# Local attention's first four tiles drawn into the last eighteen block products of the attention before it

## The reference

```
# layer 0: causal attention, 16 heads of 8
q, k, v = split(x @ W_attn + b_attn)
y = softmax(causal(q @ k.T / sqrt(8))) @ v
x = layernorm(x + y @ W_proj + b_proj)
# layer 1: two blocks of local attention, 8 heads of 64, window 64
h = shift_token(x)                       # half the channels come from the token before
q, k, v = split(h @ wqkv)
q = l2norm(q) * q_scale; k = l2norm(k) * k_scale
q, k = rotary_xpos(q, k)                 # times cos and sin tables, times a scale
o = local_attention(q, k, v)             # own window and the one before
x = x + o @ wo                           # then a gated feed-forward part
```

## Time and profile before

| | us |
|---|---|
| median of 3 runs (2395.67 to 2404.09) | 2396.33 |
| the profiled execution | 2395.39 |
| its span | 2393.6 |
| TensorE busy, share of the span | 90% |
| last `take` of the first attention starts | 210.85 |
| `v` 0 of local attention starts | 241.11 |

### The profile page before, as it was taken

How to read it: one execution, slowest core, us unless ns; L and a number is a source line. 1 busy time by engine, 2 the same in 40 slices (tenths; PEclk the granted TensorE clock), 3 DMA queues, 4 the chain that set the end, 5 groups by cost and what they waited for, 6 DMA issues and landing times.

```text
span 2393.6 us, 40349 instructions
## 1 busy us (share of the span) xinstructions
PE 2157.5 (90%) x15552; PEld 1245.5 (52%) x15552; DVE 1528.9 (64%) x3047; ACT 1140.9 (48%) x1834; POOL 747.3 (31%) x1057
## 2 busy tenths in 40 slices
PE   6886789989869888989998998999999999999988
PEld 2332456666545444545653444445666656656555
DVE  5675677787687777745556663015776776767663
ACT  2565455656514455563323555223554545545432
POOL 4544433333137765440012310003223232232133
PEclk7998899999989999999998999999999999999999
DMA  4320111111324424202012200002553553535252
GB/s 138 124 89 2 28 28 29 32 28 28 95 91 128 125 90 123 61 2 98 1 41 87 81 25 21 11 0 96 166 178 114 174 160 125 170 116 175 81 108 54
DMA packets 183975, 198.79 MB, mean 83 GB/s; under 512 B 55922, under 2 KB 152614, under 8 KB 179302
## 3 DMA queue, kind: packets, MB, share of 16 engines
q1 hardware_dynamic: 183782, 196.20, 27.2%
HBM read 93.46 MB, written 92.08 MB: 78 GB/s over the span
## 4 chain that ended last, share of the span: by engine, by line
PE 46%; DVE 5%; issue 2%; ACT 1%; DMA 1%; POOL 0%; SPq 0%; POOLq 0%; DVEq 0%; ACTq 0%
PE PS L2287 5%; PE PS L2309 5%; PE PS L2071 5%; PE PS L2294 4%; PE PS L1924 3%; PE PS L2266 2%; PE PS L1911 2%; PE PS L1914 2%; PE PS L575 2%; PE PS L2272 1%; PE PS L538 1%; PE PS L2326 1%; PE PS L557 1%; PE PS L540 1%; PE PS L2321 1%
## 5 line engine op out<-in xcount | busy, mean ns | idle before, releaser
L2432 ACT ACTIVATE AR<-PS,AR 128x512 f32<-128x512 f32 x256 | 173.7, 685 | 112.8 <-DVE AR L2370 112.8
L1253 ACT ACTIVATE AR<-PS 128x1024 f32<-128x1024 f32 x160 | 162.6, 1024 | 124.4 <-PE PS L1002 123.4
L696 ACT ACTIVATE AR<-PS 128x1024 f32<-128x1024 f32 x160 | 163.1, 1024 | 115.9 <-PE PS L561 64.1
L1106 DVE TENSOR_REDUCE AR<-PS 128x2 f32<-128x768 f32 (+1 forms) x192 | 159.9, 864 | 53.5 <-PE PS L982 27.3
L2478 POOL TENSOR_TENSOR RA<-AR,RA 128x288 f32<-128x288 f32 x128 | 89.5, 699 | 239.2 <-ACT AR L2432 239.1
L2370 DVE TENSOR_REDUCE AR<-PS 128x2 f32<-128x1024 f32 x128 | 156.8, 1225 | 11.1 <-DVE PS L2367 0.5
L2287 PE MATMUL PS<-AR 64*128 64x200 f32 (+2 forms) x1280 | 148.9, 360 | 1.9 <-ACT AR L2432 1.9
L2294 PE MATMUL PS<-CC,AR 128*128 128x128 f32 x1024 | 138.9, 279 | 0.9 <-DVE RA L2376 0.9
L2294 PEld LDWEIGHTS PS<-CC,AR 128*128 128x128 f32 x1024 | 113.6, 142 | 43.2 <-issue 39.0
L1795 POOL TENSOR_TENSOR AR<-AR 128x1024 f32<-128x1024 f32 x32 | 75.4, 2356 | 181.3 <-DVE AR L1643 181.3
L2287 PEld LDWEIGHTS PS<-AR 64*128 64x128 f32 x1280 | 104.3, 188 | 51.9 <-issue 43.3
(11 more groups left out here) (359 smaller groups left out, 5064.4 us busy)
## 6 DMA issues: line engine op xcount, KB each, us to landing
ZD<-RC SPq DMA_DIRECT2D x32, 1152.0 KB
AR<-ZD SPq DMA_DIRECT2D x32, 640.0 KB
ZP<-AR SPq DMA_DIRECT2D x128, 160.0 KB, 2.6
SP<-AR SPq DMA_DIRECT2D x40, 384.0 KB, 2.6
AR<-SP SPq DMA_DIRECT2D x128, 96.0 KB
RA<-SP SPq DMA_DIRECT2D x32, 384.0 KB
SP<-AR SPq DMA_DIRECT2D x40, 256.0 KB, 2.9
RC<-RC SPq DMA_DIRECT2D x64, 130.0 KB
```

Of the source, the lines that this page charges most:

```text
L696: e.activation(self.PT[m % 6], C.PS[:, 2 * s:2 * s + 2, :], ACT.Exp).then_inc(S["s_turned"].sem, 1)
L1106: i = e.tensor_reduce(nm[:, :, 4 * up + q:4 * up + q + 1], src[:, :, a:a + wd], AX, ALU.max, negate=True)
L1253: e.activation(self.PT[m % 6], C.PS[:, 2 * s:2 * s + 2, :], ACT.Exp).then_inc(S["s_turned"].sem, 1)
L2432: i = e.activation(self.PP[n % 5][:, hh, 16:528], C.bank[2 * (n % 2) + hh], ACT.Exp, bias=self.NMX[n % 4][:, hh:hh + 1], accum_out=self.DE ...
```

## The change

The tail of the first attention now begins at `turned` 62, so the head of local attention is spread from there to the end. `C.met` splits the mixed piece in two: eight head steps (the table products, now one step each) are dealt among the steps up to `rows` 15, the rest among what follows. "Enter" waits for nothing but the weights. In its place the first head steps wait, on each engine, for a short list (`C.prior`, method `clear`).

The `turned` steps above 70 use two pairs of banks (0 to 3), and the head's `lin` steps use two banks (4 and 5) in place of four. `init` is cut: what `lin` needs stays in it, the memsets for keys and values become a step `vals` behind "open". The buffers of the three stages are laid out anew in the same memory.

```
+            late = self.plan.index(("turned", 62))
+            self.tail = len(self.plan) - late
+            C.met[0] = self.plan.index(("rows", 15)) + 1 - late
...
-        self.slots = Turns(self.plan, 3, {"scores": S["v_scores"], "turned": S["s_turned"]})
+        self.slots = Turns(self.plan, 3, {"scores": S["v_scores"], "turned": S["s_turned"]},
+                           lambda step: range(2 if kind == 0 and step[0] == "turned" and step[1] > 70 else 3))
+        if kind == 0:
+            self.past = ()
+            C.prior = ((S["t_turned"], 69), (S["t_group"], 11, 2), (S["y_store", 0], 3), (S["y_store", 1], 3),
+                       (S["g_sb"], 3, 0), (S["g_sb"], 3, 1), (S["s_turnx"], 1), self.slots.held[2])
...
-        self.early = Turns(self.plan[:self.head], 4, {"lin": S["s_square"]})
+        self.early = Turns(self.plan[:self.head], 4, {"lin": S["s_square"]}, lambda step: (2, 3))
...
+        self.meet = (8, C.met[0])
...
-        N, plan, work = 32, [("init",), ("tabs",)], []
+        N, plan, work = 32, [("tabs", i) for i in range(8)] + [("init",)], []
...
-                plan.extend([("v", 0), ("even", 0), ("v", 1), ("even", 1)])
+                plan.extend([("vals",), ("v", 0), ("even", 0), ("v", 1), ("even", 1)])
...
         if kind == "init":
-            e.memset(self.HT[64:128, :, 64:65], 0.0)
+            self.clear(w)
+            e.memset(self.HT[64:128, :, 64:65], 0.0).then_inc(S["v_init"].sem, 1)
+        elif kind == "vals":
             e.memset(self.KT[:, :, 0:64], 0.0)
...
+    def clear(self, w):
+
+        for x in self.C.prior:
+            w.wait_ge(*x)
```

More of the change, by code:

```diff
@@ L418, in __init__ @@
         self.M0 = 48 if kind == 0 else 57
[L419 to L426, removed]
+        chunk = lambda: (bf(128, 512, 2), bf(128, 512, 2))
+        work = lambda: ([cv(128, 512) for _ in range(2)], [cv(128, 512) for _ in range(2)], [bf(128, 768, 3) for _ in range(2)])
+        rows = lambda: ([cv(128, 2, 2, 4) for _ in range(2)], [cv(16, 128) for _ in range(2)], [bf(16, 192, 3) for _ in range(2)], cv(16, 128))
+        self.CK = [None] * 5
+        if kind == 0:
+            self.CK[1], self.CK[2] = chunk(), chunk()
+            C.used = 2304
+            og = [[cv(128, 512) for _ in range(4)]]
+            self.VP = [cv(128, 64, 32), C.RC[:, 2080:4128].rearrange("p (a b) -> p a b", a=64)]
+            self.CK[3] = chunk()
+            self.FT, self.RST, self.PARTS = work()
+            C.used = 13568
+            self.PT = [cv(128, 2, 512) for _ in range(6)]
+            self.CK[0], self.CK[4] = chunk(), chunk()
+            self.NM, self.MF, self.MB, self.MR = rows()
+            assert C.used <= C.words - 4640
+        else:
+            og = [[cv(128, 512) for _ in range(4)]]
+            self.PT = [cv(128, 2, 512) for _ in range(6)]
+            self.NM, self.MF, self.MB, self.MR = rows()
+            self.CK = [chunk() for _ in range(5)]
+            self.FT, self.RST, self.PARTS = work()
+            self.VP = [cv(128, 64, 32) for _ in range(2)]
         C.used = C.words - 3136
@@ L838, in __init__ @@
         ra = lambda a, n: C.RA[:, a:a + n]
+        self.vp = cv(128, 64, 32)
         self.PARTS = [cv(128, 768).bitcast(BF).rearrange("p (a i) -> p a i", a=3) for _ in range(2)]
[L840 to L844, removed]
+        self.FT, self.LO = [cv(128, 512) for _ in range(2)], cv(128, 512)
+        assert C.used == 9472
+        qs2 = cv(128, 2048)
+        self.RST, self.TMP, self.LASTROW = [cv(128, 512) for _ in range(2)], cv(128, 512), cv(128, 16)
+        assert C.used <= 13568
         self.NMS, self.NMX = [cv(128, 4, 8) for _ in range(2)], [cv(128, 16, 4) for _ in range(2)]
         self.RD, self.QKV = cv(128, 4, 16), cv(128, 4, 128)
+        self.CK = [(queries(ra(0, 2048)), keys(ra(2048, 1024))), (queries(ra(3072, 2048)), keys(ra(n1 - 1024, 1024))),
+                   (queries(qs2), keys(cv(128, 1024))), (queries(ra(5120, 2048)), keys(cv(128, 1024)))]
         self.SUP, self.VS = [cv(128, 4, 16) for _ in range(2)], [cv(128, 4, 128) for _ in range(2)]
-        assert C.used <= C.words - 4224
-        self.vp = cv(128, 64, 32)
+        assert C.used <= C.words - 4640
         self.PT = [cv(128, 2, 512) for _ in range(6)]
@@ L1393, in __init__ @@
         self.HT, self.X1 = cv(128, NB, 576), cv(128, NB, T)
+        self.KQ = [cv(128, 1024) for _ in range(2)]
+        self.SQ, self.TQ = cv(128, 1024), [cv(128, 1024) for _ in range(2)]
+        self.KQ += [cv(128, 1024) for _ in range(2)]
         self.TB = [[cv(128, 4, 64) for _ in range(4)] for _ in range(2)]
-        self.SQ, self.TQ, self.KQ = cv(128, 1024), [cv(128, 1024) for _ in range(2)], [cv(128, 1024) for _ in range(5)]
+        self.KQ.append(cv(128, 1024))
         self.QT, self.KT = [cv(128, 4, 128) for _ in range(2)], cv(128, 4, 576)
         self.P, self.PT = [cv(128, 8, 128) for _ in range(2)], [cv(128, 8, 128) for _ in range(2)]
+        ot1 = cv(128, 512)
+        assert C.used <= C.words - 4640
+        C.used = C.words - 4640
         self.SM, self.NM = [cv(128, 4, 32) for _ in range(3)], [cv(128, 16) for _ in range(2)]
-        ot1 = cv(128, 512)
-        C.used = C.words - 4224
         self.LN, self.GR = [cv(128, 64) for _ in range(2)], cv(128, 512)
@@ L1409, in __init__ @@
             "t": {"lin": 1, "v": 1, "turnq": 1, "turnk": 1, "scores": 1, "flip": 1, "av": 1, "ot": 1, "out": 1, "two": 1, "hg": 1, "ha": 1, "four": 1, "five": 1, "turnx": 1},
-            "v": {"init": 1, "lin": 1, "sum": 1, "norm": 3, "turnk": 1, "soft": 2, "av": 2, "out": 1, "ln": 5, "two": 1, "ha": 1,
+            "v": {"init": 1, "vals": 1, "lin": 1, "sum": 1, "norm": 3, "turnk": 1, "soft": 2, "av": 2, "out": 1, "ln": 5, "two": 1, "ha": 1,
                   "four": 1, "add": 1, "fin": 5},
@@ L1419, in __init__ @@
         S["y_roll"] = C.flag("y_out", [(L,) for L in range(2 * NB)], 48)
-        self.head = self.plan.index(("v", 0))
+        self.head = self.plan.index(("vals",))
         last = self.plan.index(("out", 31)) + 1
@@ L1432, in __init__ @@
                      (S["s_turnx"], 0), (S["v_four"], 4), self.ring.held[5])
-        C.met, C.left = last - late, [(S["v_av"], 31), self.ring.held[0], self.ring.held[1]]
+        self.meet = (8, C.met[0])
+        C.met[1], C.left = last - late, [(S["v_av"], 31), self.ring.held[0], self.ring.held[1]]
     def order(self):
-        N, plan, work = 32, [("init",), ("tabs",)], []
+        N, plan, work = 32, [("tabs", i) for i in range(8)] + [("init",)], []
         def shift(n):
@@ L1658, in on_vector @@
         elif kind == "turnk":
-            w.wait_ge(S["v_init"])
+            w.wait_ge(S["v_vals"])
             w.wait_ge(S["t_scores"], n - 3)
@@ L1785, in on_gpsimd @@
         if kind == "init":
+            self.clear(w)
             e.memset(self.HT[:, :, 0:64], 0.0).then_inc(S["g_init"].sem, 1)
         elif kind == "tabs":
[L1788 to L1792, removed]
+            a, x = (("rqa", "qs"), ("rqb", "qss"), ("rka", "ks"), ("rkb", "kss"))[n % 4]
+            e.tensor_tensor(self.TB[n // 4][n % 4], W[a].rearrange("p (t d) -> p t d", t=4),
+                            W[x + str(n // 4)].unsqueeze(1).broadcast_to((128, 4, 64)), ALU.mult).then_inc(S["g_tabs"].sem, 1)
         elif kind == "sum":
```

10 lines of the change are left out of this document (6 added, 4 removed).

## The result

The changed kernel took 2410.55 us (median of 5 runs, 2405.72 to 2411.98) against 2396.33 (5 runs, 2395.67 to 2404.09): ratio 1.0043, 95% interval [1.0023, 1.0062]. That is slower, by some 10 to 14 us (10 by the ratio, 14 by the medians), where 2 us less were forecast, and outside the forecast's range. Two later measurements of the same kernel gave 2400.3 and 2401.1, so part of the 14 us is not the change's; the experiments take that up.

What follows compares the result with a forecast made beforehand. TensorE, busy 90% of the span, was taken to bound the kernel, so its idle time counts. 13.8 us saved, 11.0 spent and 0.8 for clock left 2.0 gained: median 2394.3, own range 2391.5 to 2397.5, with rivals 2386 to 2401.

Steps and rivals of the forecast that it cites:

- pause ahead of the first `lin`: TensorE newly idle for 2.8 us ahead of `lin` (0,0), while `shift` 0 waits for GpSimd's memset behind `rows` 15.
- part a: Wait of `shift` 0, then half clock up to the last product of `proj` 2: end at 204.8, before 197.94; cost 6.8 us.
- (b): From the last product of `proj` 2 to exponential 77: 10.2 us where there were 7.5; cost 2.7 us.
- (c): From exponential 77 to the end of `take` 15: 7.5 us where there were 6.0; cost 1.5 us.
- 0.8 for clock: Behind the last `take`: allowance of 0.8 us because TensorE is nearly idle and its turns may fall to half clock.
- as a block: Everything behind `v` 0 keeps its steps and order, so it should move with `v` 0, distances as before.
- 13.8 us saved behind the last `take`: From the last `take` to `v` 0: 15.9 us in place of 29.7, a saving of 13.8 us.
- 11.0 spent ahead of it: Steps inserted ahead of the last `take` make it end later: 6.8, 2.7 and 1.5, together 11.0 us.
- chain of 15.9 us: What stays behind the last `take`: sum of tile 2, `lin`, pieces, `proj`, sum 3, layer norm, turn, copy; 15.9 us.
- a sign of being wrong: Listed signs: `take` 15 less than 8 us late, no pause at first `lin`, or a later stage changed by over 2 us.
- a slower kernel: Whole kernel slower than 2408.3 us, the 0.5% limit: chance 0.03, said to have no mechanism here.
- Lockstep: Rival, chance 0.19: TensorE and ScalarE take turns, half clock from 196 to last `take`; slip 16.5, time 2400.5 us.

Runs made afterwards that it cites:

- e10: The changed kernel with 22 extra bf16 products on TensorE, results unused, in the chain behind the last `take`: 2396.63 us, 1.0010 to the kernel before.
- e9: The changed kernel measured again, unaltered: 2400.30 us (11 runs), 1.0016 to the kernel before.
- e7: The changed kernel with everything about 3 us later, by extra VectorE memsets ahead of the first copy: 2402.74 us, 1.0026 to the kernel before.
- e1: The kernel before with everything about 1 us later, by one extra VectorE memset ahead of the first copy: 2403.79 us, 1.0024 to the kernel before.
- e3: The changed kernel with everything about 1 us later, by one extra VectorE memset ahead of the first copy: 2403.34 us, 1.0037 to the kernel before.
- e6: The changed kernel with everything about 2 us later, by two extra VectorE memsets ahead of the first copy: 2402.15 us, 1.0024 to the kernel before.
- e16: The changed kernel measured for the third time, unaltered: 2401.08 us (12 runs), 1.0011 to the kernel before.
- e2: The kernel before with everything about 2 us later, by two extra VectorE memsets ahead of the first copy: 2399.99 us, 1.0008 to the kernel before.
- e5: The kernel before with everything about 3 us later, by three extra VectorE memsets ahead of the first copy: 2400.09 us, 1.0018 to the kernel before.
- e15: The kernel before, unaltered, measured as if it were a changed one: 2399.09 us (12 runs), 0.9996 to the kernel before.
- e8: The changed kernel with local attention's `init` and first shift dealt in ahead of `rows` 15, ten head steps there for eight: 2399.44 us, 1.0019 to the kernel before.

## Why the prediction was wrong

By its own steps, with the 0.5 us taken off by which the changed kernel's profile was late at the seam. Starts and ends are on the trace's clock, the other rows in us:

| step | forecast | profile after |
|---|---|---|
| pause ahead of the first `lin` | 2.8 | 2.94 |
| last product of `proj` 2 ends (part a) | 204.8 | 204.6 |
| exponential 77 starts (b) | 215.0 | 215.3 |
| `take` 15 ends (c) | 222.5 | 223.4 |
| `take` 15 to `v` 0 | 15.9, and 0.8 for clock | 18.06 |
| `v` 0 against before | -2.0 | +0.4 |
| behind `v` 0 | as a block | 5.2 lost to the first `ot`, 7.9 in layer 4 |

**Right.** The 13.8 us saved behind the last `take` and the 11.0 spent ahead of it were of the right kind and nearly of the right size: 11.6 and 12.0 measured. They cancelled, and the pause at the first `lin` that part (a) rests on is there in every profile of the changed order. The chain of 15.9 us is right to 0.1 where the clock is full: e10 takes 15.80. The close hits of the table's second and third rows are in part luck: they hold for this course of the clock. In e9 the last product of `proj` 2 ends 31.3 us behind the turn of batch 1 and not 28.0, in e7 27.4.

**Mis-sized.** "The last chain has TensorE nearly idle, so its turns may fall to half clock; I take 0.8 for that." It cost more: the last product of `proj` 3 alone went from 1.16 us (full clock) to 2.08, the turn from 0.6 to 1.09. Over the six profiles with the changed order the distance from the last `take` to `v` 0 is 17.3 to 18.1 us, 1.5 to 2.3 above e10's. So `v` 0 did not gain the 2.0: it came 0.4 late.

**Wrong.** The step that failed is "it should move with `v` 0 as a block", which put the cost of everything behind `v` 0 at nothing. The steps behind `v` 0 kept their order and their waits, but not their clock. In the profile 15.8 us were lost there (5.2 up to the first `ot`, 7.9 in layer 4, the rest in smaller pieces) against 0.4 at the seam. The prediction names such a stage behind `v` 0, longer by more than 2 us, as a sign of being wrong, and it gave a slower kernel 0.03 for want of a mechanism; the clock's course behind the seam was the mechanism. e1 shows that 8 of the 15.8 can come up without the change, and e9 that the changed kernel can be without them. The rival *Lockstep* had the sign, but not the mechanism: the slip of `take` 15 was 12.0, short of the 13.8 from which it decides. That its 2400.5 is what the repeats gave is luck.

The rule of the Trainium skill that was weighed (TensorE: Matmul & The Clock Gate, "What's actually happening": activity releases the throttle) agrees with e10, where more activity kept the full clock through the chain. Layer 4 does not fit it: there TensorE worked for 23.90 us without a pause at granted clock 0.51, and the same code left half clock sooner in other executions. The rule does not help with a forecast of where a stretch will end.

**What the change costs.** Over six profiles with its order (after, e3, e6, e7, e9, e16) and five with the old one (before, e1, e2, e5, e15), the mean from the turn of batch 1 to `v` 0 is 64.9 and 65.2 us, from `v` 0 to the first `ot` 40.7 and 39.2, from there to the end 2118.8 and 2115.5, the last scattering by more than 10 within either set. So the seam itself neither gains nor loses; 1.5 us go in the tiles behind it and about 3 in code that is the same, and these profiles cannot tell either from chance (38.7 to 43.8 against 38.6 to 41.7 in the tiles). The medians say the same: less the added delay, 2399.7 to 2402.3 for the changed kernel without its first measurement, 2396 to 2402.8 for the kernel before. The two sets overlap; the mean over all single executions is 2400.8 us for the 23 repeats of the changed kernel and 2396.9 for 157 of the kernel before. My estimate from these is that the change costs some 2 to 6 us. The other 10 of the first comparison go with the clock: the five executions had a mean granted clock of 0.949 to 0.951, the kernel before in its profile 0.959.

What stays open: why layer 4 leaves its half clock after a few microseconds in one execution and after 24 in another, why the first five runs all had the low mean clock, and whether the new layout of the buffers or the fewer banks have a share in the few microseconds that are left.

## What to carry to other kernels

Dealing the head of a stage into the tail of the one in front costs wherever an inserted step waits in a strict queue ahead of the work that bounds the tail; count what the last chain loses and what the mixture spends, since they can cancel to a microsecond, as here. Look also at what an edit of the mixture deals elsewhere: in e8 it moved a sum out of the last chain unasked. When the time moves by more than the edited place does, compare TensorE's busy time for the same count of products and the granted clock stage by stage before looking for a wait. And repeat both kernels, or displace both by a microsecond or two, before a difference under 0.5% is given to an edit.

## What the runs showed of the hardware that was not expected

The same 360 products took 38.9 us in one execution and 46.8 in another, at clock 1.00 and 0.79, with the busy time of VectorE, ScalarE and GpSimd equal to 0.2 us. The piece of layer 4 around them takes one of four lengths, 46.3, 47.6, 48.9 or 55.6 us, and nothing between, in 19 profiles. TensorE stayed at half clock (granted 0.51) through 23.90 us in which it had work without a pause, and in other executions it left half clock sooner in the same code. Medians of the same kernel differed by 2.5 us (the kernel before, 2399.09 and 2396.55 side by side) and by 10 (the changed kernel, 2410.55 and 2400.30). Extra products in TensorE's idle time (5.7 us in their rows) kept a chain at full clock and shortened it by 1.6 us, and the stretch behind it by as much.
